# A two-layer perceiver block on one core: new instruction order in both layers, another tiling of layer 1's value product, the last tile in halves, and a moved masking pass

## The reference, cut to what matters

```
x: (64 batches, 32 rows, 512), ctx: (64, 257, 512); all float32
x = x + cross_attention(layernorm(x), ctx)      # 16 heads, 4 kv heads, 96 wide
x = x + self_attention(layernorm(x))            # layer 0: 32 heads of 16, rope, causal
x = x + (layernorm(x) @ W.T + bias + lora)      # layer 0: feed-forward
# layer 1
m = top-20 mask over the 32 context rows, per batch and feature
p = layernorm(x)
gates A1, A2 = sigmoid(relu(batchnorm(conv1d([max, mean] over rows of m*p and (1-m)*p))))
x = x + m*p*A1 + (1-m)*p*A2
q, k, v = split(layernorm(x) @ w_qkv.T + b)     # 8 heads of 32
s = where(causal, k @ q.T, -10000);  a = softmax(s);  x = x + (a @ v) @ w_o.T + b_o
x = x + layernorm(x) @ (W * block_mask).T
```

## Time and profile before

| | |
|---|---|
| median of 3 timed runs | 2009.53 us (2007.81 to 2009.67) |
| the profiled execution | 2010.21 us, its span 2008.4 us |
| busy: PE, DVE, ACT, POOL | 98%, 67%, 40%, 46% of the span |
| mean granted clock of TensorE | 0.996 |

### The profile page before, as it was taken

The page is one execution under the profiler, slowest core; times in us unless marked ns, Lnnn a source line. Parts: engine busy times, 40 slices in busy tenths (PEclk is TensorE's granted clock), DMA queues, the critical chain, the costliest instruction groups (busy, mean ns, idle before and its releaser), DMA issues. The chain is left out here.

```text
span 2008.4 us, 41734 instructions
## 1 busy us (share of the span) xinstructions
PE 1965.9 (98%) x13298; PEld 1607.2 (80%) x13298; DVE 1342.3 (67%) x4410; ACT 801.3 (40%) x2285; POOL 914.7 (46%) x1522
## 2 busy tenths in 40 slices
PE   9999999999999999999999999999899999898998
PEld 7989889898988989898898989888565555575675
DVE  5846648484764849475584947557678888667875
ACT  3444435343443534344443534444233333232332
POOL 6544535354354535446453544545344444233442
PEclk9999999999999999999999999999999999999999
DMA  7100001010000001010010101010200000000000
GB/s 296 45 26 27 21 26 32 26 32 21 30 21 26 32 26 32 15 35 22 26 32 21 37 15 34 23 29 21 104 1 1 1 1 0 32 1 22 22 16 27
DMA packets 28324, 62.99 MB, mean 31 GB/s; under 512 B 14465, under 2 KB 15681, under 8 KB 27298
## 3 DMA queue, kind: packets, MB, share of 16 engines
q1 hardware_dynamic: 28194, 61.61, 9.4%
HBM read 54.15 MB, written 4.29 MB: 29 GB/s over the span
## 5 line engine op out<-in xcount | busy, mean ns | idle before, releaser
L792 ACT ACTIVATE probs<-psLane,nmax 128x289 f32<-128x289 f32 x256 | 126.2, 498 | 476.9 <-DVE nmax L914 476.9
L954 DVE MAX8 top<-work 128x8 f32<-128x257 f32 x512 | 180.0, 413 | 2.7
L492 PEld LDWEIGHTS psLane<-posT,lanes 128*128 128x128 f32 x1536 | 177.3, 192 | 4.8 <-ACT QT L781 0.6
L492 PE MATMUL psLane<-posT,lanes 128*128 128x128 f32 x1536 | 179.4, 275 | 0.4 <-ACT QT L781 0.4
L939 DVE TENSOR_TENSOR X<-X,psLane 128x512 f32 (+1 forms) x15 | 10.3, 687 | 242.0 <-PE psLane L1067 242.0
L1067 PE MATMUL psLane<-posT 128*128 128x512 f32 x384 | 167.7, 592 | 0.4 <-PEq L105 0.4
L345 POOL TENSOR_TENSOR tails<-probs,unit 128x66 f32<-128x66 f32 x128 | 38.2, 299 | 250.5 <-ACT probs L792 250.1
L767 ACT ACTIVATE w_o<-psLane 128x384 f32<-128x384 f32 (+1 forms) x256 | 113.7, 452 | 90.0 <-PE psLane L545 88.9
L565 PE MATMUL psLane<-KT,QT 96*128 96x289 f32 x512 | 146.0, 406 | 0.0
L370 POOL TENSOR_TENSOR KT<-w_qkv 128x128 f32<-128x128 f32 x64 | 29.3, 458 | 251.4 <-ACT w_qkv L739 251.4
L1067 PEld LDWEIGHTS psLane<-posT 128*128 128x128 f32 x384 | 72.4, 190 | 84.9 <-issue 84.9
(11 more groups left out here) (242 smaller groups left out, 5140.4 us busy)
## 6 DMA issues: line engine op xcount, KB each, us to landing
hid<-in_ctxT SPq DMA_DIRECT2D x64, 514.0 KB, 3.5
y<-X SPq DMA_DIRECT2D x16, 256.0 KB, 2.0
X<-in_x SPq DMA_DIRECT2D x1, 3584.0 KB, 21.4
lanes<-in_WqT SPq DMA_DIRECT2D x4, 768.0 KB, 8.6
Vtail<-Vlat SPq DMA_DIRECT2D x128, 24.0 KB
posT<-in_WoT SPq DMA_DIRECT2D x1, 3072.0 KB, 13.3
w_qkv<-in_w_qkv SPq DMA_DIRECT2D x2, 1536.0 KB, 7.0
w_ffn<-in_w_ffn SPq DMA_DIRECT2D x2, 1024.0 KB, 6.9
```

The costliest lines, as they stand in the source:

```text
L492: mm = pe.matmul(out[:, P * r:P * r + P], WqT[:, c, w:w + P], xnT[:, c, :], start=(c == 0), stop=(c == DC - 1))
L792: act.activation(probs[:, g, :], psS[:, g % 2, 0:S], ACT.Exp, bias=nmax[:, g:g + 1], scale=XSCALE, accum_out=rsum[:, j % 2, g:g + 1]).then ...
L954: ins = dve.max(top[step // 2][:, c, :], src[:, c, :] if step == 1 else work[:, c, :])
```

## The change

1. SLOTS, STARTS, OPENING and CLOSING of both layers have new numbers, and in layer 1 all engines now read OPENING and CLOSING.
2. `values` in layer 1 works in tiles of 64 rows by 32 columns: a tile holds the keys of two batches, so the probabilities are spread over two batches only (64 columns for 128, `spread_p` writes two copies for four), and there are 16 matmuls for 8. The halves go to two PSUM banks, and `evac_ot` collects them.
3. The last tile of layer 1 has `xnT2`, `ffn`, `add_ffn` and `store` in halves.
4. `mask_weights(2)` stands before the wait for the first sums in place of behind the second moment.
5. `jmask` has two more columns.

Two lines of the tables:

```diff
-    "exps": 2.342, "turn_probs": 2.461, "spread_p": 2.571, "values": 2.919, "evac_ot": 2.919,
+    "evac_v": 1.9044, "scores": 2.1102, "mask": 2.1417, "turn_probs": 2.3905, "xnT2": 2.6372, "rstd2": 2.7780,
```

The rest of the diff, cut:

```diff
@@ mix_gates, dve_program
             dve.tensor_reduce(part[:, o], conv[:, o].rearrange("p (w b) -> p w b", w=2),
                               AX.X, ALU.add).then_inc(part_done, 1)
+        mask_weights(2)
         dve.wait_ge(sums_done, 1)
...
         dve.tensor_scalar(moment[:], sums2, -1.0, EPS, ALU.mult, ALU.add).then_inc(moment_ready, 1)
-        mask_weights(2)
         dve.wait_ge(pow_done, 1)
@@ layer1
-    pT = lambda u: lanes[:, u, 1]
+    pT = lambda u: lanes[:, u, 1, 0:2 * EW].rearrange("p (h k q) -> p h k q", h=EH, k=2)
...
+            if last_tile(t):
+                for n in range(2):
+                    sp.wait_ge(s["ffn_added"], t + 1 + n)
+                    sp.dma_start(a["y"][t][:, EW * n:EW * n + EW], x_tile(t)[:, EW * n:EW * n + EW]).then_inc(out_done, 16)
...
-            for h in range(EH):
-                n, at = h // 4, L * (h % 4)
-                mm = pe.matmul(high(u)[at:at + L, P * n:P * n + P], V[:, u, L * h:L * h + L],
-                               pT(u)[:, P * h:P * h + P], start=True, stop=True, tile_position=(0, at))
+            for n in range(2):
+                for c in range(EH // 2):
+                    for half in range(2):
+                        h, lo, at = 4 * n + c, 64 * half, 512 * half + 2 * L * n
+                        mm = pe.matmul(ps[L * c:L * c + L, u, at:at + 2 * L], V[lo:lo + 64, u, L * h:L * h + L],
+                                       pT(u)[lo:lo + 64, h].rearrange("p k q -> p (k q)"), start=True, stop=True,
+                                       tile_position=(lo, L * c))
...
-            for j in range(TB):
-                ins = act.activation(pT(u).rearrange("p (h j q) -> p h j q", h=EH, j=TB)[:, :, j], v, ACT.Copy,
-                                     scale=jmask[:, j:j + 1])
+            for k in range(2):
+                ins = act.activation(pT(u)[:, :, k], v, ACT.Copy, scale=jmask[:, TB + k:TB + k + 1])
...
+            if last_tile(t):
+                for n, part in enumerate((low(u)[:, 0:EW], high(u)[:, 0:EW])):
+                    dve.wait_ge(s["ffn_filled"], t + 1 + n)
+                    half = x_tile(t)[:, EW * n:EW * n + EW]
+                    dve.tensor_tensor(half, half, part, ALU.add).then_inc(s["ffn_added"], 1)
+                return
```

More of the change, by code:

```diff
@@ L1200 @@
 SLOTS0 = {
[L1201 to L1205, removed]
@@ L1206 @@
-    "lora_down": 2.8534, "ffn": 2.8904, "lora_mask": 3.0968, "ffn_b": 3.2226, "lora_up": 3.2883, "rstd3": 3.3596,
-    "add_ffn": 3.3814, "stats3": 3.4202, "rows3": 3.6533, "turn3": 3.7101, "pos": 3.7988, "rest": 3.8757,
-    "crucial": 3.9094, "reduce_crucial": 3.9301, "reduce_rest": 3.9950,}
-SLOTS1 = {
-    "gate": 0.000, "add_rest": 0.027, "mix": 0.173, "turn_mix": 0.485, "add_mix": 0.614, "stats1": 0.707,
-    "rstd1": 0.773, "rows1": 0.929, "bias": 2.020, "turn1": 1.011, "xnT1": 1.045, "qkv": 1.310,
-    "evac_qk": 1.500, "evac_v": 1.762, "spread_k": 1.600, "scores": 2.006, "mask": 2.056, "shift": 2.136,
-    "exps": 2.342, "turn_probs": 2.461, "spread_p": 2.571, "values": 2.919, "evac_ot": 2.919,
-    "project": 3.015, "add_proj": 3.074, "stats2": 3.162, "rstd2": 3.245, "rows2": 3.395, "turn2": 3.470,
-    "xnT2": 3.539, "ffn": 3.877, "add_ffn": 3.989, "store": 3.989,}
@@ L1217 @@
[L1217 to L1224, removed]
+    "stats1": 0.0000, "rows1": 0.0372, "turn1": 0.1085, "rstd1": 0.1442, "xnT1": 0.4326, "qkv": 0.5445,
@@ new lines @@
+    "rope_sum": 0.6867, "rope": 0.6975, "turn_qk": 0.8334, "spread_k": 0.9797, "scores": 0.9837, "mask": 1.0403,
+    "spread_v": 1.2529, "shift": 1.2799, "evac_q": 1.2992, "exps": 1.5502, "total": 1.5594, "scale": 1.6138,
+    "turn_probs": 1.7080, "values": 1.8880, "project": 2.0441, "add_proj": 2.2295, "stats2": 2.2312,
+    "evac_pt": 2.2794, "rows2": 2.2814, "evac_ot": 2.3729, "rstd2": 2.4540, "turn2": 2.6258, "lora_down": 2.7453,
+    "ffn": 2.7589, "lora_mask": 2.7841, "xnT2": 2.8738, "ffn_b": 3.1922, "add_ffn": 3.2780, "stats3": 3.2877,
@@ new lines @@
+    "lora_up": 3.3187, "rstd3": 3.5871, "rows3": 3.6439, "turn3": 3.6806, "crucial": 3.8419, "rest": 3.8771,
+    "reduce_crucial": 3.8918, "pos": 3.8923, "reduce_rest": 3.9854,}
+SLOTS1 = {
+    "gate": 0.0000, "xnT1": 0.0653, "add_rest": 0.2309, "rstd1": 0.3449, "evac_qk": 0.3745, "mix": 0.4233,
+    "turn_mix": 0.6675, "add_mix": 0.7637, "bias": 0.7933, "stats1": 0.8179, "rows1": 0.8974, "turn1": 1.1088,
+    "exps": 1.1754, "spread_k": 1.2339, "qkv": 1.4746, "spread_p": 1.4878, "shift": 1.5576, "evac_ot": 1.6949,
+    "evac_v": 1.9044, "scores": 2.1102, "mask": 2.1417, "turn_probs": 2.3905, "xnT2": 2.6372, "rstd2": 2.7780,
+    "values": 2.7995, "project": 3.1361, "add_proj": 3.1818, "stats2": 3.2618, "rows2": 3.3970, "turn2": 3.6599,
+    "ffn": 3.9698, "add_ffn": 3.9950, "store": 3.9950,}
@@ new lines @@
+STARTS0 = ((0.0000, 0.9908, 1.9737, 2.9650, 3.9534, 4.9488, 5.9505, 6.9361),
+           (0.0000, 125.5506, 127.0256, 127.5583))
+STARTS1 = ((0.0000, 0.6655, 1.1114, 1.7525, 3.6961, 4.5729, 5.6317, 6.7081),
+           (0.0000, 41.2267, 37.8932, 38.7251))
+CLOSING0 = {
+    ("evac_pt", NT - 2): 128.8427, ("rstd2", NT - 2): 129.2128, ("turn2", NT - 2): 129.2872,
+    ("lora_down", NT - 2): 129.6597, ("ffn_b", NT - 2): 130.0707, ("lora_up", NT - 2): 130.1408,
+    ("reduce_rest", NT - 2): 131.3029, ("exps", NT - 1): 129.4119, ("project", NT - 1): 129.6793,
+    ("add_ffn", NT - 1): 130.9431, ("stats3", NT - 1): 131.0615,}
@@ new lines @@
+OPENING1 = {
+    ("exps", 0): 1.2463, ("add_ffn", 0): 4.1479, ("spread_k", 2): 2.1551, ("scores", 2): 3.0513,
+    ("evac_qk", 3): 2.2871, ("turn_probs", 3): 4.0389, ("gate", 4): 3.6024, ("add_rest", 4): 3.7963,
+    ("mix", 4): 4.0365, ("turn1", 4): 4.9479, ("mask", 4): 5.7444, ("project", 4): 6.6707, ("turn_mix", 5): 5.0976,
+    ("evac_ot", 5): 6.4093, ("scores", 5): 6.5658, ("values", 5): 7.4529,}
+CLOSING1 = {
+    ("add_proj", NT - 3): 38.0145, ("project", NT - 3): 39.1726, ("stats2", NT - 3): 40.0855,
+    ("turn2", NT - 3): 40.5358, ("rows2", NT - 3): 40.6192, ("ffn", NT - 3): 41.2603, ("add_ffn", NT - 3): 41.3169,
+    ("add_ffn", NT - 2): 42.2841,}
@@ L1227, in over_lanes @@
+OPENING0 = {("stats1", 1): 0.0751,}
 def over_lanes(eng, slots, starts, stages, opening_slots={}, closing_slots={}):
@@ L1751, in layer1 @@
     high = lambda u: ps[:, u, 512:1024]
+    last_tile = lambda t: isinstance(t, int) and t == NT - 1
     def sp_program(sp):
@@ L1851, in ffn @@
             pe.wait_ge(n5["xnT"], t + 1)
+            if last_tile(t):
+                for n, out in enumerate((low(u)[:, 0:EW], high(u)[:, 0:EW])):
+                    for c in range(DC):
+                        if (n, c) == (0, 2):
+                            pe.wait_ge(n5["xnT"], t + 2)
+                        mm = pe.matmul(out, xnT[:, u, c], w_ffn[:, c, EW * n:EW * n + EW], start=(c == 0), stop=(c == DC - 1))
+                    mm.then_inc(s["ffn_filled"], 1)
+                return
             for c in range(DC):
@@ L1892, in evac_ot, with evac_xnT2 @@
             act.wait_ge(s["av_filled"], t + 1)
-            act.activation(OT(u).rearrange("p n q -> p (n q)"), high(u)[:, 0:EW], ACT.Copy).then_inc(s["ot_ready"], 1)
+            act.activation(OT(u).rearrange("p n (a q) -> p a n q", a=2),
+                           ps[:, u, :].rearrange("p (a n) -> p a n", a=2)[:, :, 0:P].rearrange("p a (n q) -> p a n q", n=2), ACT.Copy)\
+                .then_inc(s["ot_ready"], 1)
         act.activation(scratch[:], neghalf[:], ACT.Exp)
         act.wait_ge(late_in, 16 * LATE_LOADS)
-        over_lanes(act, SLOTS1, STARTS1, closing_slots=CLOSING1, stages={"xnT1": evac_xnT(n4), "evac_qk": evac_qk, "exps": exps, "spread_p": spread_p,
-                                 "evac_ot": evac_ot, "xnT2": evac_xnT(n5)})
+        def evac_xnT2(t, u):
+            if not last_tile(t):
+                evac_xnT(n5)(t, u)
+                return
+            act.wait_ge(n5["xt"], t + 1)
+            act.wait_ge(s["ffn_filled"], t - LANES + 1)
+            for n in range(2):
+                act.activation(xnT[:, u, 2 * n:2 * n + 2].rearrange("p c q -> p (c q)"), high(u)[:, EW * n:EW * n + EW],
+                               ACT.Copy).then_inc(n5["xnT"], 1)
+        over_lanes(act, SLOTS1, STARTS1, opening_slots=OPENING1, closing_slots=CLOSING1, stages={"xnT1": evac_xnT(n4), "evac_qk": evac_qk, "exps": exps, "spread_p": spread_p,
+                                 "evac_ot": evac_ot, "xnT2": evac_xnT2})
     def dve_program(dve):
```

21 lines of the change are left out of this document (12 added, 9 removed).

## The result

The changed kernel takes 2015.88 us (median of 20 runs, 2010.28 to 2020.30), the kernel before in the same sessions 2008.44 (20 runs, 2006.90 to 2011.14): a ratio of 1.0031, 95% interval [1.0025, 1.0038]. The forecast was 2003.5. The spread is part of the result: before, the runs lie within 4.2 us, now within 10, and the longer a run, the lower its mean granted clock (0.997 at 2010.28 us, 0.994 at 2015.86, 0.991 at 2020.30). The profiled execution is one of the short ones: 2010.80 us, its span 2009.0.

A forecast was written before the change was run, and what follows sets the result against it. PE was taken as the bound, busy 98% of the span. From the profiled 2010.21 us, -5.0 - 1.5 - 0.5 - 7 + 12 - 4 = -6.0 gave 2004.2, as median 2003.5; its own range 1996 to 2011, with rivals 1982 to 2011.

The forecast's parts named there:

- Layer 0's loop: 13 tiles: `rows3` ends sooner and PE's wait at `turn3` goes, 0.38 us a tile, -5.0 us in all.
- The wait of 0.1: Layer 0's loop: `scale` becomes what is late, so PE still waits 0.1 us before `turn_probs`.
- Closing and gates: Layer 0's closing -1.5 us with `rows3` ahead of `add_proj`; the gates -0.5 us from the moved masking pass.
- Layer 1's opening: The new order and halved `spread_p` start layer 1's loop sooner, -7 us (0 to -10).
- Layer 1's closing: `ffn` of tile 13 fills a wait and the last tile is halved, -4 us (-1 to -5.5).
- my walk: Layer 1's closing, new order followed step by step: `add_ffn` of tile 15 ends 4.3 us sooner.
- Layer 1's loop, the mechanism: `bias` starts first, scaling takes 1.55 us, `rows2` and `mix` run beside `spread_k`: 2.1 us more a tile, 15.0, +12 in all.
- Layer 1's loop, the base: PE's own work without waits in layer 1's loop is about 12.85 us a tile, against 13.5 now.
- PE's longer waits in layer 1's loop bring its clock down: Rival, chance 0.13: a clock fall costs 1.7 us, 13.6 in all 8 tiles, giving 2017 us.
- Had the race been won: Rival, chance 0.20: in layer 1's loop DVE's scaling starts before POOL's `bias`, -5.2 for +12, giving 1985.5 us.

The follow-up runs named there:

- e9: The changed kernel with five keep-busy matmuls ahead of `turn2` alone in layer 1's loop; median 2007.15 us.
- e3: The changed kernel with five keep-busy matmuls ahead of `turn2` and five ahead of `turn_mix` in layer 1's loop; median 2008.00 us.
- e5: e1 with `bias` of tiles 4 to 7 early, seven closing keep-busy matmuls removed, tile 13's store first, layer 0's `turn1` of tile 2 moved back; 1989.13 us.
- e12: e5 with keep-busy matmuls (10, 6, 3 and 13) in four waits of PE at layer 0's edges; 1987.88 us, ratio 0.9893.
- e2: The changed kernel with one single-column POOL operation ahead of `bias` in layer 1's loop; 1998.14 us.
- e4: The kernel before with the new numbers of layer 0 alone; 2003.70 us, ratio 0.9972.
- e1: The changed kernel with POOL's `bias` directly behind `rstd1` instead of `rstd2` in layer 1's loop; 1991.86 us, ratio 0.9916.

## Why the prediction was wrong

- **Layer 0's loop**: right. 18.98 us a tile (246.71/13) for 19.30, -4.24 for -5.0. The wait of 0.1 that I had left at `turn_probs` isn't there; PE's own work is 18.98 and not 18.85.
- **Its opening**: I had nothing there and +0.97 came. It is the order: `turn1` of tile 2 now stands behind `project` of tile 0, and the `qkv` behind it waits. PE before, then now:

```profile
1452.58 3.60 PE L1185 MATMUL psLane<-w_qkv,lane_xnT 128*128 128x512 f32 x8
...
1453.58 3.70 PE L1185 MATMUL psLane<-w_qkv,lane_xnT 128*128 128x512 f32 x8 [0.69 <-ACT lane_xnT L1468]
```

The clock doesn't make the difference, since it is 0.72 from 1442 to 1448 in both profiled executions. It comes on top in both: where it held (1.00 in e9 and e3), the changed order reaches `turn_probs` of tile 1 at 1457.80 and 1458.22. e5 undid the place of `turn1` and gained nothing (1459.43), because PE then waits in two other places, 0.65 before `turn1` and 1.04 before `turn_probs` of tile 1. With the clock held, the two `turn_probs` lie 14.99 us apart in e9 and 16.02 in e12, which has this mend: it costs about 1 us, and e12 without it wasn't run.
- **Closing and gates**: right in kind, -2.49 for -1.5 and -0.38 for -0.5. But 1.6 of the 2.49 are the clock of the one execution profiled before: from `turn_probs` of tile 15 to the next `lora_down` it takes 5.01 us there, with a clock of 0.53 from 1724 to 1731, and 3.37 now at full clock. e2, with the same order and the lower clock in this place again, takes 5.07. So the order's part is nearer 0.9.
- **Layer 1's opening**: right, -7.95 for -7. 1.6 of it are `spread_p`'s, and 0.7 the lower clock at its start in the one execution profiled before: e4, with layer 1 as before, takes 91.14 for 91.83.
- **Layer 1's closing**: -2.90 for -4. All of it lies ahead of the last `turn2` (29.13 us for 32.05), where my walk had 3.8; which step of the walk gave 0.9 too much stays open. From there to the end nothing changed (8.18 for 8.16): the store of tile 13 ate the whole 0.76 of the halves, where I had booked 0.5 for them and one issue, 0.35, against them.
- **Layer 1's loop, the mechanism**: right in each step. Scaling 1.55; `rows2` ends 1.32 and `mix` 2.77 behind the start of `spread_k` (forecast 1.3 and 2.85); the two waits cost 15.25 - 13.12 = 2.13 (2.1). The trace and e1 together bear out what the Trainium skill (SBUF — State Buffer, Who interferes with whom) says of the port: the operation issued first keeps it to its end. In all eight tiles `bias` starts 2 to 5 ns ahead, and the scaling takes 1.54 to 1.55.
- **Layer 1's loop, the base**: the step "PE's own work is about 12.85" failed; it is 13.12, 2.2 us over 8 tiles. Before, `values` and `scores` stood side by side, both in tiles of 128x32; now each stands alone among full-size matmuls. After transposes the next full-size matmul starts 0.44 later, `values` 0.53 (e1's rows), `ffn` takes 3.54 us to the next start behind `values` where it is 3.43 elsewhere (1989.46 to 1992.89 in the changed kernel), and `project` 1.82 behind `scores` where it was 1.72; `values` itself is 0.06 shorter. That is 0.24 of the 0.27. Two more changes of tile size would fit it, but no run takes this apart. The prediction named the rule for it (the Trainium skill, TensorEngine Tiling (Array Packing), Key Properties: a change of mode drains the array), counted one change for two, and gave it no price.
- **The step that decided: the clock.** "PE's longer waits in layer 1's loop bring its clock down" stood there as a rival with 0.13, dismissed because layer 1's opening had 8.3 us of waits at 1.00. That reading left out the opening's first 7.9 us, which the profile of before had at 0.78, with the lower level right behind a wait of PE of 2.06 us:

```profile
1767.00:1774.90 7.90, 6.07 (x39) 5.84 (x39) 6.85 (x16) 0.93 (x3) 0.86 (x1) 0.78 0.01 3
```

Its price was right (1.7 a fall, 13.6 in all tiles), its chance wrong. In the profiled execution it cost 3.4 us, at the median about 8.5 (estimated from the two falls and the median's place above that execution; e3, less 0.9 for its longer tiles, gives 8.8). A sum of waits in an opening says little of a pair of waits that comes back every 15 us.

Against 2003.5 the median is 12.4 higher: 2.2 from the base, 8.5 from the clock in the loop, 0.7 from the profiled execution's place above the median, and 1.0 from the other stretches. Had the race been won, 1985.5 would have been wrong too: e2 with the race won is at 1998, and even without any wait in the loop (e5) the kernel is at 1989.

## What to carry to other kernels

When a new order puts an operation of POOL beside a row of DVE operations with two SBUF inputs, look for a place where DVE waits anyway or reads PSUM (here: behind `rstd1`) before judging the order as a whole: moving that one operation turned +0.3% into -0.8%. Price a wait of PE that recurs every tile with the clock as a case of its own, and look at the spread of runs beside the profile: one profiled execution showed falls in two tiles of eight. The profile of before is one execution too: 2.3 us of the gains read against it were its lower clock. Where such waits can't be removed, useless matmuls that fit into them win it back; they must be counted by their time (0.23 to 0.26 us each here), not by records.

## What the hardware showed that I had not expected

- PE is busy for 111.7 of 125.4 us in the loop and still drops to the lower clock, behind two waits of 0.90 and 0.79 us with 0.66 of transposes between, in some tiles and not in others of one execution. With either wait filled no profile shows a fall.
- Both engines of the lost race are tied to the same instant, so it was lost in all eight tiles by 2 to 5 ns, and a delay of 0.14 us on POOL only moved the collision to the next pair, whose starts then lay 0.03 us apart.
- Splitting the last tile's work into halves was worth 0.76 us, and one 256 KB store issued behind them took all of it back.
